# Attention over 4096 tokens: paired maxima, single score banks, a head's keys kept on chip

## The reference

```python
# x: [1, 4096, 256], 16 heads of 16, relative positions clipped at 64
qh = qh / math.sqrt(d)
scores = einsum('bhid,bhjd->bhij', qh, kh)
rel = clip(pos[None, :] - pos[:, None], -K, K) + K
bias = take_along_axis(einsum('bhid,rd->bhir', qh, rel_pe), rel)
attn = softmax(scores + bias, axis=-1)
out = einsum('bhij,bhjd->bhid', attn, vh)
x = layernorm(x + (out @ out_w.T + out_b))
# then two layers over windows of 128 tokens:
#   norms, rotary positions, local attention, gated feed-forward
x = layernorm(x + local_layers(x))
```

## Time and profile before

| what | us |
|---|---|
| median of three runs | 5642.28 |
| the three runs | 5639.37, 5642.28, 5642.45 |
| the profiled execution, by the clock of the runs | 5645.27 |
| its span, first to last instruction | 5643.6 |
| TensorE busy with matmuls | 5194.8 (92%) |
| VectorE busy | 4145.7 (73%) |
| ScalarE busy | 3115.0 (55%) |
| GpSimd busy | 959.2 (17%) |

### The profile page before, as it was taken

One profiled execution on the slowest core, in us unless ns is written; L12 is line 12 of the kernel. 1 busy time (PEld: TensorE's weight loads), 2 busy tenths in 40 slices (PEclk: granted clock), 3 DMA queues, 4 the chain that ended last, 5 costly groups with the idle time before them and its releaser, 6 DMA issues. The chain is left out here.

```text
span 5643.6 us, 113158 instructions
## 1 busy us (share of the span) xinstructions
PE 5194.8 (92%) x34272; PEld 2739.5 (49%) x34272; DVE 4145.7 (73%) x8689; ACT 3115.0 (55%) x4539; POOL 959.2 (17%) x711
## 2 busy tenths in 40 slices
PE   6399999999999999999999999998599989899988
PEld 3233333333333333333333333334488867788866
DVE  4288888888888888888888888871477744677755
ACT  3256666666666666666666666661266621455521
POOL 0111111111111111111111111100233310233211
PEclk7589999999999999999999999995699999999989
DMA  6612121111111221111221211111200000000000
GB/s 166 143 40 56 48 56 53 48 54 53 49 53 48 55 57 47 54 53 49 53 56 50 55 47 49 49 43 32 94 1 0 0 16 0 17 0 0 0 38 23
DMA packets 205156, 254.48 MB, mean 45 GB/s; under 512 B 72270, under 2 KB 134036, under 8 KB 203284
## 3 DMA queue, kind: packets, MB, share of 16 engines
q1 hardware_dynamic: 201220, 232.98, 14.9%
q0 software_dynamic: 3856, 20.45, 1.4%
HBM read 210.73 MB, written 42.47 MB: 45 GB/s over the span
## 5 line engine op out<-in xcount | busy, mean ns | idle before, releaser
L745 DVE TENSOR_REDUCE group_max<-shared_ps 128x1 f32<-128x512 f32 x4096 | 2684.3, 688 | 575.4 <-PE shared_ps L469 472.8
L622 ACT ACTIVATE probs<-scores 128x1024 f32<-128x1024 f32 x2048 | 2012.3, 1021 | 1042.0 <-PE scores L495 662.9
L469 PE MATMUL shared_ps<-keys,max_queries 96*128 96x512 bf16 x4096 | 1434.6, 385 | 2.0 <-issue 1.7
L495 PE MATMUL scores<-queries,keys 98*128 98x512 bf16 (+3 forms) x4096 | 1214.9, 371 | 86.6 <-ACT probs L622 85.6
L510 PE MATMUL out_ps<-probs,values 128*17 128x512 f32 x8192 | 1083.1, 601 | 0.4 <-ACT probs L622 0.4
L469 PEld LDWEIGHTS shared_ps<-keys,max_queries 96*128 96x128 bf16 x4096 | 395.6, 97 | 1116.4 <-DVE group_max L745 507.8
L215 POOL TENSOR_TENSOR near_window<-near_bias,one_f 128x1536 bf16<-128x1536 f32 x128 | 351.5, 2747 | 2942.1 <-DVE max_parts L739 2297.4
L495 PEld LDWEIGHTS scores<-queries,keys 98*128 98x128 bf16 x4096 | 359.4, 98 | 462.8 <-ACT probs L622 236.9
L521 PE MATMUL shared_ps<-block_q,block_table 96*128 96x32 bf16 x4096 | 271.5, 233 | 65.9 <-POOL block_q L406 65.9
L521 PEld LDWEIGHTS shared_ps<-block_q,block_table 96*128 96x128 bf16 x4096 | 231.3, 114 | 172.5 <-issue 123.2
L1168 POOL TENSOR_TENSOR norm<-norm,layer_expo 128x16 f32<-128x16 f32 x64 | 186.2, 2910 | 706.4 <-DVE norm L1555 706.4
(11 more groups left out here) (194 smaller groups left out, 5828.2 us busy)
## 6 DMA issues: line engine op xcount, KB each, us to landing
keys<-k_parts SPq DMA_DIRECT2D x384, 96.0 KB, 2.1
values<-v_wide SPq DMA_DIRECT2D x128, 272.0 KB, 2.8
keys<-k_parts SPq DMA_DIRECT2D x384, 64.0 KB, 2.0
keys<-k_parts SPq DMA_DIRECT2D x128, 132.0 KB, 2.4
q_stack<-part SPq DMA_DIRECT2D x96, 128.0 KB
k_parts<-part SPq DMA_DIRECT2D x96, 128.0 KB
queries<-q_stack SPq DMA_DIRECT2D x128, 96.0 KB, 2.2
max_queries<-q_stack SPq DMA_DIRECT2D x128, 96.0 KB, 2.3
```

The lines of the kernel that those rows point to most:

```text
L469: mm = pe.matmul(bank, max_queries[par][:, t * P:(t + 1) * P], keys[par][0:ROWS, (t + TPC * g) * P:(t + TPC * (g + 1)) * P], start=True, s ...
L495: mm = pe.matmul(out[:, 0:cut], keys[par][:, c * P:(c + 1) * P], queries[par][:, 0:cut], start=True, stop=True)
L622: act.activation(probs[s % 4][:], scores[s % 2][:], ACT.Exp).then_inc(exp_done, 1)
L745: dve.tensor_reduce(group_max[par][:, k:k + 1], bank, AX.X, ALU.max).then_inc(max_read, 1)
```

## The change

It changes these things:

- A pair of maxima replaces two: `max_pair` multiplies 128 queries by 2 x 512 keys into the two banks of a `max_ps`, with two matmuls of which the first has rows 0 to 47 and the second rows 64 to 113 as its contraction. Only three of the six products of parts are summed (high x high, high x middle, middle x high). Since the same maximum is subtracted from a row's scores and cancels in the softmax, it need not be exact. The keys are laid out for both uses (`KEY_COPIES`), and the scores still have all six products. VectorE's `pair_max` reduces both banks at once.
- PSUM's eight banks are now three single score banks (`score_ps`, a ring, through which the bias blocks and the rows of maxima go as well), two double ones for the maxima (`max_ps`, which the sums use too) and `out_ps`. An exponential takes one tile.
- `ORDER` mixes the near tiles with two far ones, and `near_adds` puts each add ahead of the reduction of its slot.
- A head's keys and values are loaded once, and stay for its eight steps.
- The projection stores q's parts once, has two buffers for them, and stores v three times in all, once each; its loops are written out. `head_q` is loaded by SP, at the start.
- The attention's loop holds 16 steps (two heads); the last 32 are written out.

```diff
-    SLOT_SCORES = ((0, 1), (2, 3), (), ())
-    NEAR_SLOTS = (26, 27, 30, 23)
-    ROWS_SLOT = 20
+    PAIRS_M = 16
+    LEAD = 10
+    ORDER = [5, 0, 1, 6, 2, 3, 7, 4] + list(range(8, TILES))
+    ROWS_TURN = 4
+    RING = 3
+    MAX_ROWS = slice(6 * D, 6 * D + MROWS)
+    KEY_ROWS = MAX_ROWS.stop + D
+    KEY_COPIES = ((0, 2, 0), (0, 1, 2 * D), (2, 3, 3 * D), (0, 2, P // 2), (0, 1, MAX_ROWS.stop))
+    UPPER, LOWER = slice(0, 3 * D), slice(P // 2, KEY_ROWS)
...
-        scores = [ps(f"scores{i}", [P, 2, CH]) for i in range(2)]
-        shared_ps = [ps(f"shared_ps{i}", [P, CH]) for i in range(3)]
+        score_ps = [ps(f"score_ps{i}", [P, CH]) for i in range(RING)]
+        max_ps = [ps(f"max_ps{i}", [P, 2, CH]) for i in range(2)]
...
-                mm = pe.matmul(bank, max_queries[par][:, t * P:(t + 1) * P],
-                               keys[par][0:ROWS, (t + TPC * g) * P:(t + TPC * (g + 1)) * P],
-                               start=True, stop=not near)
+                for b, rows in enumerate((UPPER, LOWER)):
+                    mm = pe.matmul(banks[:, b, :], max_queries[par][rows, t * P:(t + 1) * P],
+                                   keys[key_par][rows, (first + 4 * b) * P:(first + 4 * b + 4) * P],
+                                   start=True, stop=not NEAR_PARTS.get((j, b)))
...
+                def free(at):
+                    pe.wait_ge(score_read, items_before(m, i, at - 2))
+                    return score_ps[at % RING][:]
+
+                for turn in range(QUADS):
+                    pv_quad(m, i, turn)
+                    if turn == ROWS_TURN:
...
+                    for half in range(2):
+                        slot = 2 * turn + half
...
+                            pe.wait_ge(max_read, max_before(m, i, slot - 1))
+                            max_pair(*later(m, i, ahead), (slot + LEAD) % PAIRS_M, M_START + i * M_ITEMS + slot)
+                        for k in range(2):
+                            pos = (4 * (turn + 2) + 2 * half + k)
+                            if pos < TILES:
+                                score(m, i, pos, free(at))
...
-                act.activation(probs[s % 4][:], scores[s % 2][:], ACT.Exp).then_inc(exp_done, 1)
+                act.activation(probs[:, pos % 8, :], bank, ACT.Exp).then_inc(score_read, 1)
...
-                dve.tensor_reduce(group_max[par][:, k:k + 1], bank, AX.X, ALU.max
-                                  ).then_inc(max_read, 1)
+                dve.tensor_reduce(group_max[i % 2][:, t, j:j + 1], max_ps[item % 2][:], AX.XY, ALU.max
+                                  ).then_inc(max_read, 1)
...
+                for slot in range(PAIRS_M):
+                    near_adds(m, i, last, slot // 2, slot % 2)
...
+                        pair_max(*later(m, i, ahead), (slot + LEAD) % PAIRS_M, M_START + i * M_ITEMS + slot,
+                                 max_before(m, i, slot + 1))
...
-                dve.memset(keys[i][ROWS:ROWS + MROWS, :], 1.0).then_inc(ident_ready, 1)
+                dve.memset(keys[i][MAX_ROWS, :], 1.0).then_inc(ident_ready, 1)
...
+                if i % CHUNKS == CHUNKS - 1 and (not last or n + 1 < TOTAL - CHUNKS):
+                    load_keys(head_of(m, i) + 2, i // CHUNKS)
+                    sp.wait_ge(pv_done, at_step(m, i, QUADS, QUADS + 2))
+                    load_values(head_of(m, i) + 2, i // CHUNKS)
```

And in `project_heads`:

```diff
-                    if unit < 2:
-                        for t, which in enumerate(Q_PARTS):
-                            sp.dma_start(q_stack[heads, t * D:(t + 1) * D, bass.ds(col, CH)],
-                                         part[:, which, v, :]).then_inc(parts_stored[v], 16)
...
-                for again in range(2):
-                    sp.dma_start(v_wide.rearrange("h p (t e) -> p h t e", e=VW)
+                    for which in range(3):
+                        sp.dma_start(parts[heads, which * D:(which + 1) * D, side:side + CH],
+                                     part[:, par, which, v, :]).then_inc(parts_stored[par], 16)
+                if n in V_SPANS:
+                    sp.wait_ge(v_staged, n + 1)
```

More of the change, by code:

```diff
@@ new lines, in max_before, with rows_placed, at_step @@
+    def max_before(m, i, slot):
+        whole = at_step(m, i, M_ITEMS, M_START + slot)
+        if not isinstance(m, int):
+            return whole
+        n = m * BODY + i
+        gone = sum(n * M_ITEMS + slot > k * M_ITEMS + late for k, late in ABSENT)
+        return whole - gone
+    def rows_placed(m, i):
+        if isinstance(m, int) and m == 0 and i == 0:
+            return 2 * NEXT_GEN + 1
+        return items_before(*later(m, i, -1), STEP.index(("rows", 0))) + 1
+    def at_step(m, i, per, plus):
+        return m * (BODY * per) + (i * per + plus)
@@ L234, in attend, with later @@
+    def later(m, i, ahead):
+        over = (i + ahead) // BODY
+        return m + over, i + ahead - over * BODY
     with ExitStack() as ctx:
@@ new lines, in _, with step @@
+            copy_window(0, 2, 0)
+            def step(m, i, last):
+                n = m * BODY + i
+                if not last or n + NEXT_GEN + 2 < TOTAL:
+                    copy_block(m, i + NEXT_GEN + 2, items_before(m, i, 1 + STEP.index(("bias", 1))))
+                if not last or n + 3 < TOTAL:
+                    bias = items_before(*later(m, i, 1), 1 + STEP.index(("bias", 1)))
+                    copy_window(*later(m, i, 3), bias)
+            with pool.Fori(0, LOOPED) as m:
+                for i in range(BODY):
+                    step(m, i, False)
```

853 lines of the change are left out of this document (424 added, 429 removed).

## The result

The changed kernel takes **5763.64 us** (median of four runs, 5759.92 to 5792.69; two more took 5773.86 and 5788.96), the kernel before in the same job 5642.36: a ratio of 1.0229 (95% interval 1.0197 to 1.026). The forecast was 5676 in a range of 5440 to 5800. So the sign and the range held and the size did not. The profiled execution is the slowest of the four, 5792.69 us, 29 above the median.

What follows compares the result with a forecast made beforehand. It took TensorE, by a little, to bound the first attention's plain turns. Steps +128 us, less 4 for the nine without bias, projection -90: +34 us, so 5676 us on the median, range 5440 to 5800.

Steps and rivals of the forecast that it cites:

- Projection: Stage before the attention, bound by SP's DMA stores: 15 us a chunk instead of 26.3, -90 us over eight chunks.
- Change of shape: TensorE switching between matmuls using different parts of the array: 0.10 us each, five in a plain turn instead of two.
- A pair: Two halved maxima matmuls on TensorE, alone behind a switch: 0.27 us, about 0.05 of it the second's exposed weight load.
- Plain turn: Turns 2 to 5 of an attention step: 2.78 us each against 2.82, the pairs' gain nearly all given back to switches.
- Bias turns: Turns 0 and 1, where a bias block waits for a score bank: 4.05 us each, +0.39 us a step together.
- Turns 6 and 7: Near-diagonal tiles: adds wait behind longer reductions, out_copy and the sums come late; 8.35 us instead of 7.57, +0.78 us.
- The step: One of the first attention's 128 steps (head and chunk): -0.16 + 0.39 + 0.78 = +1.0 us.
- The loops now hold 16 steps ... I put that at nothing: Attention's longer loop and 32 straight steps: claimed to cost nothing, since no row shows the code's arrival as a wait.
- serial pairs: Rival: a pair's two matmuls follow each other, 0.43 us a pair, 2.1 us a step: 5945 us, chance 0.12.
- free row switches: Rival: row switches cost nothing for the bf16 pairs, plain turn 2.38 us: 5456 us, chance 0.14.
- a reduction that gains nothing: Rival: VectorE's reduction over two banks takes 1.38 us, 0.4 us a step more: 5727 us, chance 0.16.
- Halves that start together: First rival: a pair's two matmuls start together, 0.22 us instead of 0.27, 0.6 us a step: 5600 us, chance 0.18.

Runs made afterwards that it cites:

- e3: The changed kernel with the two pairs of maxima of a turn placed next to each other, between the scores: 5693.91 us, ratio 1.0114 to the kernel before.
- e6: The kernel before with all 128 attention steps written out in straight code, nothing else changed: 5605.99 us, ratio 0.9912 to the kernel before.
- e1: The changed kernel with all 128 steps of the first attention written out, no loop: 5571.15 us, ratio 0.989 to the kernel before.
- e4: The changed kernel with both matmuls of a pair on the same half of the array's rows, same result: 6593.08 us, ratio 1.1698 to the kernel before.
- e7: The changed kernel in straight code, with the two pairs of a turn next to each other: 5732.35 us, ratio 1.013 to the kernel before.
- e12: Kernel e7 with TensorE's wait before the sums filled by three matmuls whose result nobody reads: 5500.38 us, ratio 0.9738 to the kernel before.
- e10: The changed kernel in straight code, with ScalarE's copy to out_copy two exponentials earlier: 5650.16 us, ratio 0.9996 to the kernel before.
- e5: The kernel before with its attention loops' bodies widened from 2 steps to 16: 5689.58 us, ratio 1.0055 to the kernel before.
- e2: The changed kernel with the next head's keys and values loaded two steps into a head, not at its end: 5737.59 us, ratio 1.0179 to the kernel before.

## Why the prediction was right in sign and wrong in size

- *Projection*, -90: right, -85.
- *Change of shape*, 0.10 us each: right (0.32 from pair to score, e3's -0.59 us).
- *A pair*, 0.27: 0.05 too much. Both halves start together, as the first rival had it.
- *Plain turn*, 2.78: right in sum, by two errors that cancel. The pairs won 0.10 and the last score's wait for a bank lost about as much. The text called that bank "just in time"; it is late.
- *Bias turns*, 2 x 4.05: right, 4.01 and 4.02. *Reductions*, 1.22: right.
- *Turns 6 and 7*, 8.35: mechanism right (near adds behind reductions, `out_copy` late), 0.29 too long. The sums started at 7.07 us and not at 7.25, and took 0.99 and not 1.1. They waited 0.66 us, not over 1, as TensorE itself was done only at 6.4, where 6.0 was forecast.
- *The step*, +1.0: measured +0.31 undisturbed, +0.09 with both kernels in straight code. Of the 0.7 us missed, turns 0, 1, 6 and 7 make 0.36 (16.09 us where 16.45 was forecast). The rest lies in turns 2 to 5, which took 12.21 us (27.49 less 7.71 and 7.57) and take 11.71: -0.50, where one of the four, priced four times, gave -0.16. Two of the twelve matmuls with `near_window` moved from there to turn 1 (0.06 us each), and turn 3, which has four of them before and after, went from 3.06 to 2.93 us: with them in it the last score doesn't come late, and the pairs' gain shows.
- *"The loops now hold 16 steps ... I put that at nothing"*: **this step failed.** "No row shows the code's arrival as a wait" was true of a profile with loops of two steps, and says nothing of a longer body. It cost 67 us at the jumps, and what the loop adds inside a step, 0.43 us in the changed kernel, was in the old one too, at 0.21 (e6). With the slow clock that went with it the loop's form is worth 3.3% (e1).
- *The clock* was in no term. The forecast priced every step at full clock, as nearly all steps before have it, and foresaw the longer waits in front of the sums without asking what they do to the clock. It cost 123 us in the loop's steps. That kind of cost decides the result: of the kernels here, the order by undisturbed step is not the order by time.

The rivals: serial pairs are refuted by e4, free row switches by the 0.32 us, and a reduction that gains nothing by 1.218 us. Halves that start together came true as a fact, but not its 5600 us. That the range held was luck, because two misses partly cancel: the step's +1.0 us, 0.7 too much over some 120 steps (83 us), against 190 us of jumps and slow clock that weren't seen. "A wait that I don't see" was named as what would make it wrong, for the plain turn; it stood elsewhere.

## What to carry to other kernels

Before a matmul-bound loop is tuned by tenths of a microsecond, look at the granted clock in windows, and at where in the step TensorE has several short waits in a row: filling one of 0.6 us a step was worth 4% here (e7 and e12), three times its own length, while shortening it made one kernel worse (e10). Keep a loop body short or write it out; the middle, a body of 16 steps, had the costs of both here. Most of a gain or loss credited to an edit of the body may be the loop's, so time the old body in the new loop form as well (e5, e6).

## What the runs showed of the hardware

- A jump back over 16 steps of code made its step 7.4 to 10.3 us longer in the old kernel (e5), 3.24 and 1.04 us of it TensorE's waits at the first jump. In the changed kernel TensorE stood 12.01 us with 1.8 MB of keys in flight, of which 2.28 remained when these were moved (e2).
- TensorE's clock fell from 2.4 to 1.2 GHz behind waits of 0.17, 0.21 and 0.58 us between busy stretches (e7), for some 10 us each time, and not once in the attention with the last wait filled (e12). It fell five times, for 3.4 us each, in the kernel before, which has no wait right ahead of the sums. The Trainium skill (TensorE: Matmul & The Clock Gate, "A second HAM failure mode: psum-queue depth-cycling") tells of a kernel whose short pauses between groups of matmuls made the clock swing. The trace agrees.
- In e4 the pair's halves follow each other on the same rows, TensorE is busy for longer, and the clock falls more often than in any other kernel (83 falls with 1338 us between 300 and 3700 us). No run here explains it.
